# Late tiles of a routed feed-forward layer scattered into the output, and the low weights of experts 0 and 1 made by other engines

## The chip, the cores and the metric

The program runs on one core of a Trainium2 chip. The metric is the device time of one execution in microseconds; 1149.94 us is the median of three runs before the change (1149.91 to 1152.03).

## What is computed

One pre-norm decoder layer, all float32, for x of 4 x 512 x 256 tokens: a selective-scan mixer, a cross-attention over 4 x 1601 context rows, and a mixture of eight experts of which each token takes two. The change touches the last part alone, apart from two small stores.

```
scores = xt @ Wg.T                       # 2048 tokens, 8 experts
topk_scores, topk_idx = top_k(scores, 2)
y_e = (silu(xt @ W1_e.T) * (xt @ W2_e.T)) @ W3_e.T      # hidden width 704
out = x + sum over the two chosen e of score_e * y_e
```

## The kernel before, in words

The program has two parts with a barrier of all engines between them. `mixer_phase` does the mixer and the attention, batch by batch, in an order written out by hand. At its end the normalised tokens of a batch are stored to DRAM (`store_tokens`, line 303), the router's product is copied into `scores` (line 692), and SyncE waits for the stores (line 335). Near its start 5 MB of zeros are written to the DRAM tensor `ffn_sorted` (lines 269 and 270).

`routed_ffn_phase` sorts the 4096 (token, expert) pairs into 39 tiles of 128 rows, each tile of one expert, and works through the tiles. It has these pieces.

Routing. SyncE loads the weights of experts 0 and 1 (`load_expert`), ScalarE rounds each to `w_hi` (line 1236). Meanwhile VectorE runs a chain of small instructions, each of which waits for the one before (`chain`): the two best experts of each token, the place of each pair in the sorted order (`pos_f`), and one-hot matrices `place_row` and `place_tile` (lines 1335 to 1343), from which TensorE makes by 32 products the token number of each sorted row (line 1447, `tok_id`). The one-hot matrices lie in the space of `w_lo`, the low parts of the weights. So `w_lo` of expert 0 is made by VectorE only behind the routing (`split_rest(0)`, line 1394), and that of expert 1 behind the first tile's product (`split_rest(1)`). Each has a part of 2816 and one of 1536 columns.

Gathers. GpSimd fetches the 39 tiles of tokens with one indirect DMA each (line 1180). Tiles 0 to 3 are read from `tok`, later ones after a copy by SyncE into `tok_in` (`load`, line 1100), issued four tiles ahead right behind the store of a tile.

Tiles. For tile i TensorE transposes the tokens, makes gate and up products in three float32r products each (line 1478), transposes the hidden rows (lines 1487 and 1491) and makes the down product (line 1503); tile i + 1's gate and up stand in front of tile i's down. ScalarE rounds and applies silu, VectorE makes the low parts (lines 1373, 1381), the product (1367) and the copy of the result out of PSUM (`evacuate`, line 1388). SyncE stores each result to `ffn_sorted` (line 1109). The loops of TensorE, ScalarE, VectorE and SyncE are hardware loops over pairs of tiles or groups of eight.

Later experts. Behind the gathers, GpSimd waits for the last tile of expert e, makes `w_hi` and `w_lo` of expert e + 2 (lines 1151 and 1154), and issues the load of expert e + 4 (`reload`, line 1088). For experts 2 and 3 the loads are issued by SyncE, once `w_lo` of experts 0 and 1 is there.

End. A token's two rows lie at a lower and a higher place. Once all tiles up to the last of expert 6 are stored, GpSimd gathers the 16 blocks of lower rows (`fetch(y_one, 0, ...)`, line 1195); once tile 38 is stored, it gathers the 16 blocks of upper rows. VectorE multiplies each by its score and adds it to `x_all` (lines 1425, 1430), and SyncE stores pairs of blocks (line 1132).

## Time and profile before

| | |
|---|---|
| median of three runs | 1149.94 us |
| profiled execution, span from first to last instruction | 1151.0 us |
| TensorE busy over the span | 928.8 us (81%) |
| VectorE, ScalarE, GpSimd busy | 669.2, 445.6, 590.9 us |
| chain that ended last, by engine | PE 24%, DVE 3%, DMA 2%, POOL 1% |
| mean granted TensorE clock | 0.885 |

The page gives no time of the profiled execution beside its span; the span stands 1.06 us above the median. The part with the experts begins at 789 us. In the stretches of the profile PE is TensorE, PEld its weight loads, DVE VectorE, ACT ScalarE, POOL GpSimd and SP SyncE. POOL's busy time holds its making of DMA descriptors for indirect DMAs; a DMA's own time is "to landing".

### The profile page before, as it was taken

The page shows a single profiled execution, that of the slowest core. Times are in us where ns is not written, and L with a number is a line of the kernel's source. Part 1 is how long each engine was busy: PE and PEld are TensorE (multiplying, and loading weights), DVE is VectorE, ACT ScalarE, POOL GpSimd, SP SyncE. Part 2 cuts the span into 40 slices and gives each one's busy share as a digit, 9 for nine tenths or more (in the row PEclk, how much of TensorE's full clock was granted, in tenths as well). Part 3 has the DMA queues.
Part 4 walks back from the last instruction along what each step waited for, and adds up shares of the span by engine and source line. Part 5 has one row for each costly group of instructions (what it writes and reads, how often), then busy time and mean ns, then how long its engine had stood idle before and what let it go on. Part 6 is the DMA issues. An engine that isn't in the chain of part 4 may idle for free. (4 is left out here: it accounts for less than half of the span.)

```text
span 1151.0 us, 16215 instructions
## 1 busy us (share of the span) xinstructions
PE 928.8 (81%) x5148; PEld 731.9 (64%) x5149; DVE 669.2 (58%) x1097; ACT 445.6 (39%) x827; POOL 590.9 (51%) x481
## 2 busy tenths in 40 slices
PE   5767677889877889885989877992699999999970
PEld 2344345457666546665657765672689899999970
DVE  4189777697457788547677872416634343443443
ACT  2455754355544445635345530322222222222210
POOL 2176675755446565546576743110578553335505
PEclk9869877899886899996899987995699999999995
DMA  9440030000044000026000040004365312311304
GB/s 322 161 175 1 1 111 37 1 15 1 1 163 132 1 9 7 1 75 220 1 8 8 1 147 1 15 1 169 123 207 127 125 48 100 112 36 36 109 19 146
DMA packets 48954, 85.44 MB, mean 74 GB/s; under 512 B 6292, under 2 KB 38696, under 8 KB 46856
## 3 DMA queue, kind: packets, MB, share of 16 engines
q1 hardware_dynamic: 43032, 65.77, 17.0%
q0 software_dynamic: 5872, 19.02, 5.7%
q8 instruction: 29, 0.48, 0.2%
q14 instruction: 21, 0.17, 0.0%
HBM read 65.64 MB, written 14.55 MB: 70 GB/s over the span
## 5 line engine op out<-in xcount | busy, mean ns | idle before, releaser
L373 POOL TENSOR_TENSOR u<-dtx,b_all 128x512 f32<-128x512 f32 x256 | 326.6, 1288 | 212.9 <-DVE h L620 209.7
L620 DVE TENSOR_TENSOR_SCAN h<-da,u 128x512 f32<-128x512 f32 x256 | 308.6, 1217 | 136.8 <-ACT da L455 89.5
L455 ACT ACTIVATE da<-dt_,a_neg 128x512 f32<-128x512 f32 x256 | 174.8, 689 | 133.3 <-DVE h L620 132.5
L746 PE MATMUL ysum<-ident,h 128*128 128x128 f32 x1024 | 159.3, 301 | 57.9 <-DVE h L620 44.5
L746 PEld LDWEIGHTS ysum<-ident,h 128*128 128x128 f32 x1024 | 132.5, 156 | 104.2 <-DVE h L620 56.8
L924 PE MATMUL pv<-pT,ctx_n 128*128 128x128 f32 (+1 forms) x832 | 109.5, 288 | 7.6 <-DVE x_all L681 7.6
L924 PEld LDWEIGHTS pv<-pT,ctx_n 128*128 128x128 f32 (+1 forms) x832 | 104.6, 204 | 10.8 <-DVE x_all L681 9.1
L895 PE MATMUL pa<-ctx_t,xnT_a 128*128 128x401 f32 (+1 forms) x256 | 97.3, 508 | 13.9 <-DVE sim L602 12.6
L1367 DVE TENSOR_TENSOR hid<-act_,ps_u 128x352 f32<-128x352 f32 x78 | 40.6, 521 | 86.8 <-ACT act_ L1221 86.8
L1221 ACT ACTIVATE act_<-ps_g 128x352 f32<-128x352 f32 x78 | 36.3, 466 | 104.2 <-PE ps_u L1478 104.2
L1503 PE MATMUL ps_y<-w_hi,hidT_hi 128*128 x234 | 70.9, 303 | 2.7 <-DVE hidT_lo L1381 2.7
L895 PEld LDWEIGHTS pa<-ctx_t,xnT_a 128*128 128x128 f32 x256 | 44.9, 192 | 44.2 <-DVE sim L602 19.2
L729 PE MATMUL pm<-xnT_m,w_in 128*128 128x512 f32 x128 | 65.1, 637 | 6.3 <-DVE xs L576 4.8
L1503 PE MATMUL ps_y<-w_lo,hidT_hi 128*128 x234 | 66.5, 284 | 0.0
L1503 PE MATMUL ps_y<-w_hi,hidT_lo 128*128 x234 | 66.3, 283 | 0.0
L1226 ACT CAST hidT_hi<-ps_h 128x512 fp32r<-128x512 f32 x39 | 22.9, 586 | 104.3 <-PE ps_h L1491 100.1
L1180 POOL DMA_INDIRECT tok<-xn_dram,tok_id x39 | 43.9, 1125 | 35.3 <-DVE tok_id L1349 23.7
L1381 DVE TENSOR_TENSOR hidT_lo<-ps_h,hidT_hi 128x512 fp32r<-128x512 f32 (+2 forms) x117 | 42.1, 415 | 34.1 <-ACT hidT_hi L1226 34.1
L602 DVE COPY_PREDICATED sim<-mask,pa 128x401 f32<-128x401 uint8 x64 | 38.0, 596 | 37.1 <-PE pa L895 37.1
L1154 POOL TENSOR_TENSOR w_lo<-w_raw,w_hi 128x2816 fp32r<-128x2816 f32 (+1 forms) x12 | 58.6, 4882 | 0.0
L1478 PE MATMUL ps_g<-w_hi,tokT_hi 128*128 x156 | 54.6, 350 | 3.4 <-issue 3.3
L1162 POOL TENSOR_TENSOR pool_scrap<-ident 128x1 f32<-128x1 f32 x26 | 4.8, 193 | 96.3 <-PE ps_y L1503 85.3
(216 smaller groups left out, 1780.5 us busy)
## 6 DMA issues: line engine op xcount, KB each, us to landing
b_all<-b_dram SPq DMA_DIRECT2D x16, 1024.0 KB, 4.6
ctx_t<-in_ctxT SPq DMA_DIRECT2D x4, 1601.0 KB
ctx_n<-in_ctx SPq DMA_DIRECT2D x4, 1536.0 KB
ffn_sorted<-yg SPq DMA_DIRECT2D x1, 4992.0 KB, 22.5
ffn_sorted<-y_sb SPq DMA_DIRECT2D x39, 128.0 KB
tok_in<-tok SPq DMA_DIRECT2D x35, 128.0 KB, 2.0
mask<-in_mask SPq DMA_DIRECT2D x16, 200.1 KB, 2.4
w_raw<-in_w1T SPq DMA_DIRECT2D x4, 704.0 KB, 4.2
```

The costliest lines, as they stand in the source:

```text
L373: nc.gpsimd.tensor_tensor(u[:, i % 2, :], dtx[:, j % 2, :], b_all[:, n, :], ALU.mult).then_inc(u_ok, 1)
L455: nc.scalar.activation(da[i % DS][:], dt_[:, j % 2, :], ACT.Exp, scale=a_neg[:, j, n:n + 1]).then_inc(da_ok, 1)
L620: nc.vector.tensor_tensor_scan(h[:, i % HS, :], da[i % DS][:], u[:, i % 2, :], 0.0, ALU.mult, ALU.add).then_inc(scan_ok, 1)
L729: last = nc.tensor.matmul(bank[:], w_in[:, k, j * P:(j + 1) * P], xnT_m[:, k, :], start=k == 0, stop=k == KD - 1)
L746: last = nc.tensor.matmul(ysum[:, t * P:(t + 1) * P], h[:, i % HS, t * P:(t + 1) * P], ident[:], is_transpose=True, start=n == 0 and t == ...
L895: last = nc.tensor.matmul(pa[c % 2][:, 0:hi - lo], xnT_a[:, k, q * P:(q + 1) * P], ctx_t[:, k, lo:hi], start=k == 0, stop=k == KD - 1)
L924: last = nc.tensor.matmul(pv[:, k * P:(k + 1) * P], ctx_n[0:w, c, k * P:(k + 1) * P], pT[0:w, c, :], start=c == 0 and k == 0, stop=c == KC ...
L1154: nc.gpsimd.tensor_tensor(w_lo[:, p * NW + lo:p * NW + hi], w_raw[:, p, lo:hi], w_hi[:, p * NW + lo:p * NW + hi].bitcast(F32), ALU.subtrac ...
L1180: pool.indirect_dma_start(tok[:, i, :], None, xn3_dram, bass.IndirectOffsetOnAxis(ap=tok_id[:, i:i + 1], axis=0)).then_inc(tok_ld[i // 2 % ...
L1381: nc.vector.tensor_tensor(hidT_lo[0:rows_in, c:c + n, :], bank[0:rows_in, col:col + n * P].rearrange("p (c m) -> p c m", m=P), hidT_hi[0:r ...
L1478: last = nc.tensor.matmul(out[:, 0:HH], x[:, p, k * P:(k + 1) * P], w[:, at(e % 2 * NW + (first + k * HF), HH)], start=k == 0 and n == 0, ...
L1503: last = nc.tensor.matmul(ps_y[:, 0:D], x[0:rows_in, c, :], w[0:rows_in, at(e % 2 * NW + (2 * NGU + c * D), D)], start=c == 0 and n == 0, ...
```

## The change

It has these parts.

1. **Early and late tiles.** Tiles 0 to 29 are early, 30 to 38 late (`LATE = 9`). Early results go to `ffn_sorted` as before. Late results stay in `y_late` in SBUF.
2. **The scores weigh the rows.** Each token's eight scores are stored behind its 256 values in DRAM (`store_scores`, once per batch), and the gather of tokens brings them along (rows of 264 values). VectorE makes from them one weight per sorted row (`tile_masks`, `row_weights` for tiles 0 to 7 before the first result is copied out, for tiles 8 to 38 before that of tile 8) and multiplies by it while it copies a result out of PSUM. Row 0 of that DRAM tensor is zero and serves the unused rows.
3. **Early rows are added by the DMA.** Behind the store of tile 29, GpSimd issues 16 + 16 indirect DMAs that add rows of `ffn_sorted` to `x_all`. Rows that belong to late tiles are replaced by 128 rows of zeros. SyncE stores pairs of blocks to the output when both of a pair's additions have landed.
4. **Late rows are scattered.** When all eight stores have landed, GpSimd scatters late tiles from SBUF with addition into the output in DRAM: 8 DMAs for the lower rows, 9 for the upper, of which an upper one waits until the lower ones of the tiles before it have landed. Rows that don't take part go to spare rows behind the output. VectorE makes the row numbers before it copies out tile 9 (`late_rows`).
5. **Placement buffers.** `place_row` gets a buffer of its own, whose space the late buffers use afterwards, and `place_tile` lies in `hidT_hi` and `hidT_lo`.
6. **Low weights.** GpSimd makes `w_lo` of expert 0 as soon as ScalarE has rounded each part. VectorE makes that of expert 1 between the tokens of tile 0 and those of tile 1.
7. VectorE's loop over the tiles is written out; the zeros written at the start are 128 rows in place of 4992.

```diff
+LATE = 9
...
+    EARLY = NT - LATE
+
+    ffn_sorted = nc.dram_tensor("ffn_sorted", [(EARLY + 1) * P, D], F32).ap()
+    xn3_dram = nc.dram_tensor("xn3_dram", [G * P + 1, D + E], F32).ap()
...
-                sp.dma_start(env["ffn_sorted"].rearrange("(n p) d -> p n d", p=P),
-                             zeros.unsqueeze(1).to_broadcast([P, NT, D])).then_inc(res_st, 16)
+                sp.dma_start(env["ffn_sorted"][EARLY * P:(EARLY + 1) * P, :], zeros[:, 0:D]).then_inc(res_st, 16)
+                sp.dma_start(xn3_dram[0:1, :], zeros[0:1, :]).then_inc(res_st, 16)
...
+                        sp.dma_start(xn3_dram[at(b * S + t * P + 1, P), 0:D], xn[:, t, :]).then_inc(tok_st, 16)
+
+                def store_scores(b):
+                    sp.wait_ge(r_ok, b + 1)
+                    sp.dma_start(xn3_dram[at(b * S + 1, S), D:D + E].rearrange("(t p) e -> p t e", p=P),
+                                 scores[:, b * T:(b + 1) * T, :]).then_inc(score_st, 16)
...
+                        store_scores(b - 1)
+                store_scores(B - 1)
                 sp.wait_ge(tok_st, 16 * B * T)
+                sp.wait_ge(score_st, 16 * B)
...
+        tok = sb("tok", [P, NT, D + E])
...
+        with ExitStack() as placing:
+            place = buf(placing, "place", [P, 2 * G * P], F32R)
+        place_row = place[:].rearrange("p (k g m) -> p k g m", k=2, g=G)
+        place_tile = [t[:].rearrange("p c m -> p (c m)")[:, 0:G * COLS].rearrange("p (g t) -> p g t", g=G)
+                      for t in (hidT_hi, hidT_lo)]
+
+        y_late = sb("y_late", [P, LATE, D])
...
+        BATCHES = [range(LATE - 3)] + [range(t, t + 1) for t in range(LATE - 3, LATE - 1)]
+        low_st, high_st = [sem(f"low_st{n}") for n in range(len(BATCHES))], sem("high_st")
+        KNOWN = 8
...
-                for i in range(LAST, NT - AHEAD):
+                for i in range(LAST, EARLY):
                     store_and_load(i, i % GROUP)
-                for i in range(NT - AHEAD, NT):
-                    store(i, i % 2)
-                out = io["out"].rearrange("(g p) d -> p g d", p=P)
+                for i in range(EARLY, NT - AHEAD):
+                    sp.wait_ge(y_ok2, i + 1)
+                    load(i + AHEAD, (i + AHEAD) % GROUP)
+                out = io["out"][0:G * P, :].rearrange("(g p) d -> p g d", p=P)
-                    sp.wait_ge(comb, G + g + 2)
+                    sp.wait_ge(both_ld[g // 2], 64)
                     sp.dma_start(out[:, g:g + 2, :], x_all[:, g:g + 2, :]).then_inc(out_st, 16)
...
+                def split_rest(e):
+
+                    for n, (lo, hi) in enumerate(PARTS):
+                        pool.wait_ge(hi_ok, 2 * e + n + 1)
+                        nc.gpsimd.tensor_tensor(w_lo[:, e * NW + lo:e * NW + hi], w_raw[:, e, lo:hi],
+                                                w_hi[:, e * NW + lo:e * NW + hi].bitcast(F32), ALU.subtract).then_inc(w_ok, 1)
+
+                split_rest(0)
...
-                def fetch(y, k, done):
-                    for g in range(G):
-                        pool.indirect_dma_start(y[:, g, :], None, ffn_sorted,
-                                                bass.IndirectOffsetOnAxis(ap=pos[:, k, g:g + 1], axis=0)).then_inc(done(g), 16)
+
+                def add_early(k, g):
+                    pool.indirect_dma_start(x_all[:, g, :], None, ffn_sorted,
+                                            bass.IndirectOffsetOnAxis(ap=pos[:, k, g:g + 1], axis=0),
+                                            compute_op=ALU.add).then_inc(both_ld[g // 2], 16)
+
+                def add_late(k, t, done):
+                    pool.wait_ge(y_ok2, EARLY + t + 1)
+                    pool.indirect_dma_start(io["out"], bass.IndirectOffsetOnAxis(ap=late_to[:, k, t:t + 1], axis=0),
+                                            y_late[:, t, :], None, compute_op=ALU.add).then_inc(done, 16)
 
                 pool.wait_ge(pos_ok2, 1)
-
                 for p in range(2):
-                    stores = pool.value_load(tile_end[0:1, E + p:E + p + 1], min_val=1, max_val=NT)
-                    pool.wait_ge(y_st[p], stores * 16)
-                    take_wait()
-                fetch(y_one, 0, lambda g: low_ld)
-
-                for p in range(2):
-                    pool.wait_ge(y_st[p], so_far(NT - 1 if (NT - 1) % 2 == p else NT - 2, p))
-                fetch(y_two, 1, lambda g: up_ld[g // 2])
+                    pool.wait_ge(y_st[p], so_far(EARLY - 1 if (EARLY - 1) % 2 == p else EARLY - 2, p))
+                for g in range(G):
+                    add_early(0, g)
+                for g in range(G):
+                    pool.wait_ge(both_ld[g // 2], 32)
+                    add_early(1, g)
+
+                pool.wait_ge(late_ok, 1)
+                pool.wait_ge(out_st, 16 * (G // 2))
+                for n, batch in enumerate(BATCHES):
+                    for t in batch:
+                        add_late(0, t, low_st[n])
+                    if n == 0:
+                        pool.wait_ge(low_st[0], 16 * len(BATCHES[0]))
+                    else:
+                        pool.wait_ge(low_st[n - 1], 16 * len(BATCHES[n - 1]))
+                    for t in batch:
+                        add_late(1, t, high_st)
+                pool.wait_ge(low_st[len(BATCHES) - 1], 16)
+                add_late(1, LATE - 1, high_st)
+                pool.wait_ge(high_st, 16 * LATE)
...
-                chain(nc.vector.tensor_tensor(first[:, 0, :], pos_f[:, 0, :], pos_f[:, 1, :], ALU.is_lt))
-                chain(nc.vector.tensor_scalar(first[:, 1, :], first[:, 0, :], -1.0, 1.0, ALU.mult, ALU.add))
-                nc.vector.tensor_copy(pos[:], pos_f[:]).then_inc(pos_ok2, 1)
...
-                    chain(nc.vector.tensor_tensor(w_part[:, 0, :], w_top[:, 0, :], first[:, k, :], ALU.mult))
-                    chain(nc.vector.tensor_tensor(w_part[:, 1, :], w_top[:, 1, :], first[:, 1 - k, :], ALU.mult))
-                    chain(nc.vector.tensor_tensor(w_low[:, k, :], w_part[:, 0, :], w_part[:, 1, :], ALU.add))
+                    chain(nc.vector.tensor_scalar(is_late[:, k, :], pos_f[:, k, :], float(EARLY * P), None, ALU.is_ge))
+                    chain(nc.vector.tensor_scalar(to_zero[:, k, :], pos_f[:, k, :], num_f[:, 0:1], float(EARLY * P - 1),
+                                                  ALU.subtract, ALU.subtract))
+                    chain(nc.vector.tensor_tensor(to_zero[:, k, :], to_zero[:, k, :], is_late[:, k, :], ALU.mult))
+                    chain(nc.vector.tensor_tensor(pos_f[:, k, :], pos_f[:, k, :], to_zero[:, k, :], ALU.subtract))
+                nc.vector.tensor_copy(pos[:], pos_f[:]).then_inc(pos_ok2, 1)
...
-                    nc.vector.tensor_copy(y_sb[:, p, :], ps_y[:, 0:D]).then_inc(y_ok2, 1)
+                    if i < EARLY:
+                        wait(dve, y_st[p], so_far(i - 2, p))
+                    y = y_sb[:, p, :] if i < EARLY else y_late[:, i - EARLY, :]
+                    nc.vector.tensor_scalar(y, ps_y[:, 0:D], w_row[:, i:i + 1], None, ALU.mult).then_inc(y_ok2, 1)
+
+                def tile_masks():
+                    shape = [P, NT, E - 1]
+                    chain(nc.vector.memset(above[:, :, 0:1], 1.0))
+                    chain(nc.vector.memset(above[:, :, E:E + 1], 0.0))
+                    chain(nc.vector.tensor_tensor(above[:, :, 1:E], iot_f[:, 0:NT].unsqueeze(2).to_broadcast(shape),
+                                                  tend[:, 0:E - 1].unsqueeze(1).to_broadcast(shape), ALU.is_ge))
+                    chain(nc.vector.tensor_tensor(w_tile[:], above[:, :, 0:E], above[:, :, 1:E + 1], ALU.subtract))
+
+                def row_weights(lo, hi):
+                    for n in range(PAIRS):
+                        last = max(i for i in range(hi) if i // 2 % PAIRS == n)
+                        dve.wait_ge(tok_ld[n], gathered(last))
+                    chain(nc.vector.tensor_tensor(w_tile[:, lo:hi, :], w_tile[:, lo:hi, :], tok[:, lo:hi, D:D + E], ALU.mult))
+                    chain(nc.vector.reduce_sum(w_row[:, lo:hi], w_tile[:, lo:hi, :], AX_X))
+
+                def late_rows():
+                    own, late = tok[:, EARLY:NT, D:D + E], above[:, EARLY:NT, :]
+                    chain(nc.vector.tensor_scalar(low_s[:], late[:, :, 1:E + 1], OUT_OF_WAY, -OUT_OF_WAY, ALU.mult, ALU.add))
+                    chain(nc.vector.tensor_tensor(low_s[:], low_s[:], own, ALU.add))
+                    chain(nc.vector.scalar_tensor_tensor(out=high_s[:], in0=late[:, :, 0:E], scalar=-OUT_OF_WAY, in1=own,
+                                                         op0=ALU.mult, op1=ALU.add))
+                    chain(nc.vector.reduce_max(low_max[:], low_s[:], AX_X))
+                    chain(nc.vector.reduce_max(high_max[:], high_s[:], AX_X))
+                    chain(nc.vector.tensor_copy(row_id[:], tok_id[:, EARLY:NT]))
+                    chain(nc.vector.tensor_scalar(taken_by[:, 0, :], row_id[:], 1.0, None, ALU.is_ge))
+                    chain(nc.vector.tensor_tensor(taken_by[:, 1, :], low_max[:], high_max[:], ALU.is_ge))
...
+                    for k in range(2):
+                        chain(nc.vector.tensor_scalar(dump[:, k, :], num_f[:, 0:LATE], float((G + k * LATE) * P - 1), None, ALU.add))
+                        chain(nc.vector.scalar_tensor_tensor(out=away[:, k, :], in0=row_id[:], scalar=-1.0, in1=dump[:, k, :],
+                                                             op0=ALU.add, op1=ALU.subtract))
+                    chain(nc.vector.tensor_tensor(away[:], away[:], taken_by[:], ALU.mult))
+                    chain(nc.vector.tensor_tensor(away[:], away[:], dump[:], ALU.add))
+                    nc.vector.tensor_copy(late_to[:], away[:]).then_inc(late_ok, 1)
 
...
-                split_rest(0)
                 rest_of_tokens(0, 0)
+                split_rest(1)
                 rest_of_tokens(1, 1)
                 multiply(0, 0)
-                split_rest(1)
...
-                dve.wait_ge(low_ld, 16 * G)
-                for g in range(G):
-                    nc.vector.scalar_tensor_tensor(out=x_all[:, g, :], in0=y_one[:, g, :], scalar=w_low[:, 0, g:g + 1],
-                                                   in1=x_all[:, g, :], op0=ALU.mult, op1=ALU.add).then_inc(comb, 1)
-                for g in range(G):
-                    dve.wait_ge(comb, g + 1)
-                    dve.wait_ge(up_ld[g // 2], 32)
-                    nc.vector.scalar_tensor_tensor(out=x_all[:, g, :], in0=y_two[:, g, :], scalar=w_low[:, 1, g:g + 1],
-                                                   in1=x_all[:, g, :], op0=ALU.mult, op1=ALU.add).then_inc(comb, 1)
+
+                rest_of_hidden(0)
+                rest_of_tokens(2, 0)
+                multiply(1, 1)
+                tile_masks()
+                row_weights(0, KNOWN)
+                for i in range(NT):
+                    if i > 0:
+                        rest_of_hidden(i)
+                        if i + 2 < NT:
+                            rest_of_tokens(i + 2, i % 2)
+                        if i + 1 < NT:
+                            multiply(i + 1, (i + 1) % 2)
+                    if i == KNOWN:
+                        row_weights(KNOWN, NT)
+                    if i == KNOWN + 1:
+                        late_rows()
+                    evacuate(i, i % 2)
```

## Rows read from the trace of the kernel before

**Rows 1.** The windows view: busy PE, PEld, DVE, ACT, POOL; PEclk, DMA share, GB/s.

```profile
810.00:820.00 10.00, 4.01 (x18) 3.52 (x18) 8.03 (x18) 0.37 (x1) 5.45 (x3) 0.50 0.09 26
950.00:1000.00 50.00, 49.09 (x342) 46.95 (x341) 19.62 (x48) 14.47 (x42) 17.21 (x12) 1.00 0.32 113
```

**Rows 2.** The timeline of SyncE's queue; start, duration. The last row merges tiles 35 to 38.

```profile
1054.99 0.34 SPq L1109 DMA_DIRECT2D ffn_sorted<-y_sb  x1
...
1097.96 21.13 SPq L1109 DMA_DIRECT2D ffn_sorted<-y_sb  x4
```

**Rows 3.** The timeline of all engines, at the end of the program.

```profile
1118.31 0.42 DVE L1388 COPY y_sb<-ps_y 128x256 f32<-128x256 f32 x1 [4.26 <-PE ps_y L1503]
...
1120.72 1.22 POOL L1195 DMA_INDIRECT tok<-ffn_sorted,pos  x1 [35.44 <-DMA ffn_sorted<-y_sb]
...
1128.70 18.12 SPq L1132 DMA_DIRECT2D out<-x_all  x8
...
1142.60 0.96 POOL L1195 DMA_INDIRECT tok<-ffn_sorted,pos  x1 [0.30 <-issue]
```

**Rows 4.** The timeline where the second part of the program begins.

```profile
788.47 0.19 DVE L692 COPY scores<-pv 128x32 f32<-128x32 f32 x1 [5.68 <-PE pv L942]
788.94 0.38 SPq L1077 DMA_DIRECT2D w_raw<-in_w1T  x1
```

**Rows 5.** The view of DMAs: KB of each, median us from issue to landing.

```profile
out<-x_all SPq DMA_DIRECT2D x8, 256.0 KB, 2.3
...
tok<-xn_dram,tok_id POOLq DMA_INDIRECT x39, 5.2
...
w_conv<-in_w_conv SPq DMA_DIRECT2D x1, 8.0 KB, 9.6
...
tok<-ffn_sorted,pos POOLq DMA_INDIRECT x16, 2.9
```

**Rows 6.** The timeline of the routing and of the first tokens.

```profile
797.28 3.91 ACT L1236 CAST w_hi<-w_raw 128x2816 fp32r<-128x2816 f32 x2 [12.48 <-DMA w_raw<-in_w3T]
...
800.29 0.29 DVE L1317 TENSOR_TENSOR eq<-oh,slot 128x128 f32<-128x128 f32 x1
...
811.09 0.17 DVE L1347 TENSOR_TENSOR w_low<-w_part 128x16 f32<-128x16 f32 x1
...
813.45 0.20 DVE L1349 CAST tok_id<-ps_y 128x39 uint32<-128x39 f32 x1 [1.56 <-PE ps_y L1447]
...
815.90 4.74 DVE L1394 TENSOR_TENSOR w_lo<-w_raw,w_hi 128x2816 fp32r<-128x2816 f32 x2
816.64 4.83 POOL L1180 DMA_INDIRECT tok<-xn_dram,tok_id  x1 [0.30 <-issue]
...
818.93 0.37 ACT L1215 CAST tokT_hi<-ps_x 128x256 fp32r<-128x256 f32 x1 [9.70 <-PE ps_x L1465]
820.57 0.41 DVE L1373 TENSOR_TENSOR tokT_lo<-ps_x,tokT_hi 128x256 fp32r<-128x256 f32 x1
```

**Rows 7.** The timeline in the mixer, VectorE beside GpSimd.

```profile
347.60 1.26 POOL L373 TENSOR_TENSOR u<-dtx,b_all 128x512 f32<-128x512 f32 x1 [1.23 <-DVE h L620]
347.61 1.27 DVE L228 TENSOR_TENSOR ln_t<-ln_t,ln_var 128x4 f32<-128x4 f32 x1
```

**Rows 8.** The timeline of GpSimd: expert 2's first, expert 7's last low weights.

```profile
872.45 6.27 POOL L1154 TENSOR_TENSOR w_lo<-w_raw,w_hi 128x2816 fp32r<-128x2816 f32 x1
...
1050.88 3.51 POOL L1154 TENSOR_TENSOR w_lo<-w_raw,w_hi 128x1536 fp32r<-128x1536 f32 x1
```

**Rows 9.** The timeline of VectorE at expert 1's low weights and at tile 8.

```profile
829.65 4.75 DVE L1394 TENSOR_TENSOR w_lo<-w_raw,w_hi 128x2816 fp32r<-128x2816 f32 x2
...
898.52 0.42 DVE L1388 COPY y_sb<-ps_y 128x256 f32<-128x256 f32 x1 [1.43 <-PE ps_y L1503]
```

**Rows 10.** The chain of waits behind tile 0's product; start, duration.

```profile
838.34 0.44 DVE y_sb L1388
...
839.57 7.43 DMA tok_in<-tok
```

78 lines of the change are left out of this document (34 added, 44 removed).

## The prediction, made before the changed kernel ran

> **What bounds the kernel now.** The page's slices come first: TensorE is busy 9 tenths or more in nearly every slice of the expert part, with two holes, one where that part begins and one at the end. The windows view gives the same by stretch: among the tiles TensorE works 49.09 of 50 us at a granted clock of 1.00, in the routing 4.01 of 10 us at 0.50 [rows 1]. So the tiles are TensorE's, one each 7.16 us ((1097.96 - 1054.99) / 6, tile 29 to 35 [rows 2]), and the change touches no product. The timeline of the end shows the second hole: the last result leaves PSUM at 1118.31, and from 1120.72 to the end at 1151.0 GpSimd's making of 16 gathers, one each 1.26 us (0.96 and 0.30 idle), is the bound [rows 3]. The first hole is VectorE's chain from 789 to `tok_id` at 813.45, and from there to the first tile [rows 6]. Those two holes are what the change works on, and the sum is one over their edges.
>
> **The barrier between the parts.** Before, the second part starts 0.28 us after the scores' copy ends (788.66 to 788.94 [rows 4]). Now the last batch's scores are stored first and the barrier waits for their landing: 512 pieces of 32 bytes. No row shows this store. A store of 256 KB in whole rows lands in 2.3 us, and a load of 512 pieces of 16 bytes, queued behind others at the start, took 9.6 [rows 5]. I take 3.0, nearer the store, as nothing else is in flight: +3.1 with the issue, bounds +1.7 (a landing under the store's, since 16 KB is little) and +9.7. The Trainium skill (DMA: Bandwidth & Descriptors, Specifications) asks for 512 bytes a piece and says that below it the DMA reads, modifies and writes; that speaks for the upper half of this range, and no row here shows it for a store.
>
> **The routing.** GpSimd now runs `w_lo` of expert 0 while VectorE is in its chain: 6.27 and 3.51 us [rows 8], from 799.8 on, when ScalarE's first cast ends (797.28 and 2816/4352 of its 3.91 us [rows 6]). In the mixer a product of GpSimd from 347.60 to 348.86 stands beside a VectorE instruction of four elements a row with two inputs in SBUF, started at 347.61: it took 1.27 us and ended with GpSimd's [rows 7], where a link of 16 elements took 0.17 [rows 6]. So a VectorE instruction with two inputs in SBUF waits for the whole of a GpSimd instruction that reads SBUF, and most of the chain is of this form. Step by step: GpSimd takes the first part at 799.94, between two chain links, until 806.2; the link of 800.29 [rows 6] ends at 806.5 in place of 800.58 (+5.9). GpSimd's second part goes in behind that link, 806.5 to 810.0; VectorE only has a reduction (0.29) to do meanwhile, which has one input, and the next link ends 8.6 later than before. That gives +9.0 with the two links that the change takes out there (0.21 each) put back in; net of these and of the copy to `pos`, which moves behind, +8.5 for `tok_id`. The new chain links behind the one-hot matrices (8 small ones for 6, about 0.2 us each by the 0.17 of 811.09 [rows 6]) lie beside TensorE's last 16 placing products. Bounds: 0, if the two run side by side without loss, and +9.8, both parts in full.
>
> This is also where the Trainium skill speaks against the change. SBUF — State Buffer, Who interferes with whom, says that a VectorE instruction with two SBUF inputs contends with a GpSimd one that reads SBUF, and that whoever starts first keeps the shared port for its whole instruction. By that rule the step costs the 8.5 above; if each only slowed the other to half its speed, VectorE would lose some 4 to 5 in those 9.8 us. Rows 7 agree with the rule.
>
> **From `tok_id` to the first tiles.** Before, ScalarE had the tokens of tile 0 rounded at 819.30, but VectorE was in `split_rest(0)` until 820.57 [rows 6]: -1.25 with that gone. Before, `split_rest(1)` of 4.75 us [rows 9] stood between tile 0's product and its low hidden parts, and held back the first down product; now it lies beside the first gate and up products, and all its dependants but `rest_of_tokens(1)` come later than its end: another -0.85 net, so -2.1 by tile 0's result. It holds back GpSimd's gathers, as `split_rest(0)` did (4.83 for 0.96 [rows 6]), but these run ahead of their tiles.
>
> Loads follow `w_lo`. Expert 2's load now starts about 12 us ahead of the first gather and is over by it; it used to run beside the gathers. Expert 3's was issued behind `split_rest(1)`, at 834.4 (829.65 and 4.75 [rows 9]), so that the copy of tile 4's tokens, issued 839.57, took 7.43 us behind it [rows 10], and TensorE, back at 844.6 (a pitch of tiles behind tile 0), waited until 847.0. Now that load is issued about 11 us ahead of tile 0's result and over when the copy is issued, which then takes the 2 to 3 us it has elsewhere: -2.4. If it still collides, 0. The same collision near tile 9 is tied to the ends of tiles and stays.
>
> **Among the tiles.** The weighted copy out of PSUM has the shape of the old copy, 0.42 us, and reads one input from PSUM: 0. `tile_masks` and `row_weights(0, 8)` are 6 links, some 1.8 us, ahead of tile 0's result, where VectorE has 1.4 us idle behind its products [rows 9] and the next down product is 4 us off (gate and up of the next tile lie between): 0. `late_rows` is 17 links of about 0.2, so 3.5 us, in a place with the same 1.4 us idle and 4 us to TensorE's next need; GpSimd's second part for expert 3 (3.51) may hold its first link by 1.1. I take +0.5, bounds 0 and +4 (it also delays the copy of tile 13's tokens into a load). Storing the scores of earlier batches waits on SyncE ahead of a mask load that is due a third of a batch later, and the 5 MB of zeros ran beside products that waited for nothing of it: both 0. So TensorE's last tile shifts by 3.1 + 8.5 - 2.1 - 2.4 + 0.5 = +7.6.
>
> **The end.** In times of before: tile 29's store is issued at 1054.99 [rows 2]; with the 1.96 us between tile 38's store and its first gather (1118.76 to 1120.72 [rows 3]), the additions start at 1056.95. 32 at 1.26 are 40.3: 1097.3. No row shows an addition. I take GpSimd's price of a gather (0.96 and 0.30), and 4 us to land, between the 2.9 and 5.2 of the two kinds of gather [rows 5]. The last addition lands at 1100.0, its pair's store of 2.3 at 1102.8; at 1103 the scatters start. None of them can go earlier, though tiles 30 to 35 lie ready, so part of the work that was behind the last tile still is. 6 lower ones take until 1110.6, the last lands at 1113.3; 6 upper until 1121.1; lower and upper of tile 36 and lower of 37 until 1124.9; the wait for tile 36's landing and the upper of 37 until 1126.5; the last waits until 1127.8 for the lower of 37, and lands at 1132. The old tail from the landing of the last store to the end is 2.3 (18.12 after 1128.70, less a store's own 0.37, plus 2.3, against 1151.0 [rows 3, 5]): 1134.2, so -16.8. TensorE's last result, 1118.3, is 9 us off this path, which hangs on tile 29 alone; every shift of tile 29 passes through in full.
>
> **Sum.** 7.6 - 16.8 = -9.2 on the span of 1151.0, 1141.8; as the span stands 1.06 above the median, 1140.7: 1141 us.
>
> **Rivals.**
> A, as summed: 1141, with its own range 1136 to 1147. Chance 0.45.
> B, GpSimd and VectorE work side by side in the routing, if its short links and their gaps let both in: -8.5 more, 1132. For it: the granting among so short instructions isn't in any row. Against: rows 7. Chance 0.13.
> C, slower. GpSimd's making of an adding DMA is dearer than of a gather, as a destination must be read too. 49 of them stand in one chain, so an extra of 0.19 us each (9.2 / 49) eats the gain. The first gather of a group took 1.22 for 0.96 [rows 3]; at that price 49 x 0.26 = +12.7, 1153. For it: no adding DMA in the trace, and nothing in the chain has slack. Against: each moves the same 128 rows. Chance 0.23.
> D, landings are longer, 5.2 or more, since an addition reads and writes DRAM. Four stand bare (last early one, batch of six, tile 37's lower, last): 4 x 1.2 = +5, 1146; at twice that 1150. Chance 0.14.
> E, the change does not do what it says at the end: GpSimd still with expert 7's parts when tile 29 is stored (1050.88 and 3.51 [rows 8] is only 2.6 us ahead of 1056.95), or a store of small pieces near 9.6. Either alone +3 to +7: 1144 to 1148. Chance 0.05.
>
> The range that holds 8 in 10 is 1129 to 1154, from B with a better tail to C. About 0.2% (2.3 us) is what can be told from no change. A, B and E are faster, C is slower but for its cheap quarter, D is split: faster 0.75, same 0.06, slower 0.19.
>
> **What would show it.** The scores' store ahead of the second part, its first instruction about 792. VectorE instructions of 6 and 3.5 us among the chain beside GpSimd's line of `w_lo`; `tok_id` about 825, or 816.6 under B. Tile 0's result about 848, and no wait for tile 4's tokens. 32 additions on GpSimd at 1.26 from 1065, then a gap of 5 to 6 us, and a program that ends some 16 us behind TensorE. The prediction is wrong if the additions' pitch is above 1.45, or if the chain's links keep their 0.3 us beside GpSimd.

## The result, and the profile after it

The change makes the kernel slower: 1170.97 us (median of 4 runs, 1169.72 to 1172.12) against 1149.93 (median of 4, 1149.69 to 1152.03), a ratio of 1.018 with a 95% interval of 1.0165 to 1.0194. The prediction was 1141, faster, with a range up to 1154. The profiled execution took 1172.12 and spans 1170.4, against 1151.0 before: +19.4 is what the rows have to explain. The profiles used here differ by up to 2.6 us in when the first part of the program ends, also where the code up to there is the same, so the sums below are taken over stretches inside one profile.

First the page of the changed kernel, its span and its groups of GpSimd's indirect DMAs (columns: count, busy us, mean ns of one, idle time of the engine before them), with the chain that ended last ahead of the groups and the median us to landing behind them.

```profile
span 1170.4 us, 15966 instructions
...
POOL 3%; issue 1%; DMA 1%; POOLq 0%
POOL out L1240 2%; POOL x_all L1234 1%; DMA out<-y_late,late_to 1%; POOLq L1239 0%
...
L1234 POOL DMA_INDIRECT x_all<-ffn_sorted,pos x32 | 50.0, 1562 | 12.4 <-issue 9.4
L1219 POOL DMA_INDIRECT tok<-xn_dram,tok_id x39 | 40.2, 1030 | 23.7 <-DVE tok_id L1404 12.1
...
x_all<-ffn_sorted,pos POOLq DMA_INDIRECT x32, 3.8
out<-y_late,late_to POOLq DMA_INDIRECT x17, 3.7
```

Both kinds in the top groups are indirect DMAs of 128 rows from GpSimd's queue. The 39 that only gather take 1.03 us on average; the 32 that also add (L1234) take 1.56. The chain holds nothing but the adding ones. The timeline of the end shows the same in order (start us, us, engine, line; idle before in brackets):

```profile
1061.05 0.34 SPq L1139 DMA_DIRECT2D ffn_sorted<-y_sb  x1
...
1063.64 1.71 POOL L1234 DMA_INDIRECT x_all<-ffn_sorted,pos  x1 [2.98 <-DMA ffn_sorted<-y_sb]
...
1121.50 1.56 POOL L1234 DMA_INDIRECT x_all<-ffn_sorted,pos  x1 [0.30 <-issue]
...
1123.05 0.48 DVE L1445 TENSOR_SCALAR y_late<-ps_y,w_row 128x256 f32<-128x256 f32 x1 [2.95 <-PE ps_y L1584]
...
1128.60 1.60 POOL L1240 DMA_INDIRECT out<-y_late,late_to  x1 [5.54 <-issue]
...
1142.08 1.55 POOL L1240 DMA_INDIRECT out<-y_late,late_to  x1 [2.56 <-DMA out<-y_late,late_to]
...
1161.04 1.55 POOL L1240 DMA_INDIRECT out<-y_late,late_to  x1 [0.70 <-DMA out<-y_late,late_to]
```

One addition every 1.86 us (1.56 and 0.30 idle) where a gather came every 1.26 [rows 3]. The 32 additions last from 1063.64 to 1123.06. By then TensorE's last result is leaving PSUM (1123.05 against 1118.31 [rows 3]), and all 17 scatters are still to come: 47.4 us stand between that result and the end (1170.4), where before there were 32.7 (1151.0 - 1118.31).

The first hole, in the timeline of the routing; the counterparts are [rows 4, 6]:

```profile
787.43 0.19 DVE L703 COPY scores<-pv 128x32 f32<-128x32 f32 x1 [5.68 <-PE pv L953]
787.65 0.37 SPq L314 DMA_DIRECT2D xn_dram<-scores  x1
789.88 0.38 SPq L1107 DMA_DIRECT2D w_raw<-in_w1T  x1
...
801.25 9.63 POOL L1192 TENSOR_TENSOR w_lo<-w_raw,w_hi 128x2816 fp32r<-128x2816 f32 x2 [10.09 <-ACT w_hi L1293]
801.55 0.29 DVE L1375 TENSOR_REDUCE pos_f<-eq 128x16 f32<-128x128 f32 x1
801.87 5.67 DVE L1377 TENSOR_TENSOR w_part<-pos_f 128x16 f32<-128x16 f32 x1
807.57 3.35 DVE L1378 TENSOR_TENSOR pos_f<-pos_f 128x16 f32<-128x16 f32 x1
...
822.48 0.20 DVE L1404 CAST tok_id<-ps_y 128x39 uint32<-128x39 f32 x1 [0.73 <-PE ps_y L1528]
```

The reduction at 801.55, one input, runs beside GpSimd in its usual 0.29 us. The next two links have two inputs in SBUF and 16 elements a row each, and take 5.67 and 3.35. They end at 807.54 and 810.92. The row of `w_lo` merges GpSimd's two instructions, and the view of the tile `w_lo` parts them (shortest, median and longest in ns, first and last start):

```profile
L1192 POOL TENSOR_TENSOR w_lo<-w_raw,w_hi x2: 3424/4838/6252, 801.3 to 807.5; 128x2816 fp32r<-128x2816 f32 x1, 128x1536 fp32r<-128x1536 f32 x1
```

The first lasts 6.25 from 801.25, to 807.50, the second until 810.88 (801.25 and 9.63): each link ends as one of them ends. The second part of the program starts 0.94 later than before (789.88 against 788.94), and `tok_id` is made 9.03 later.

### The profile page after: what moved, and what is told of

It reads as the page before. It is cut to its first block and busy times, and to the rows that moved or that the text cites. A ratio compares the mean times of both kernels' runs of the same rounds, so it can differ in the third digit from the quotient of the medians.

```text
span 1170.4 us, 15966 instructions
## 1 busy us (share of the span) xinstructions
PE 928.0 (79%) x5148; PEld 730.3 (62%) x5149; DVE 670.2 (57%) x1088; ACT 445.3 (38%) x827; POOL 638.8 (55%) x498
## 5 line engine op out<-in xcount | busy, mean ns | idle before, releaser
L740 PE MATMUL pm<-xnT_m,w_in 128*128 128x512 f32 x128 | 67.9, 660 | 5.7 <-DVE xs L588 4.3
L1234 POOL DMA_INDIRECT x_all<-ffn_sorted,pos x32 | 50.0, 1562 | 12.4 <-issue 9.4
L1219 POOL DMA_INDIRECT tok<-xn_dram,tok_id x39 | 40.2, 1030 | 23.7 <-DVE tok_id L1404 12.1
```

What stands on the lines that cost most here:

```text
L740: last = nc.tensor.matmul(bank[:], w_in[:, k, j * P:(j + 1) * P], xnT_m[:, k, :], start=k == 0, stop=k == KD - 1)
L1234: pool.indirect_dma_start(x_all[:, g, :], None, ffn_sorted, bass.IndirectOffsetOnAxis(ap=pos[:, k, g:g + 1], axis=0), compute_op=ALU.add). ...
```

## The experiments

The first question is whether the price of an addition on GpSimd makes the end longer (theory P), or something that stays when the additions are gone (Q, as its expectation puts it). A second group asks whether the routing's delay is GpSimd's hold on the two-input links. A third uses what was found. The kernels without the additions, with halves, with the low weights behind the routing and with the low weights in the gap ran on one chip, where the kernel before took 1153.66 us (7 runs, 1148.13 to 1155.51). The other four ran on a second one (1149.58, 10 runs, 1147.07 to 1153.07). The changed kernel itself was run on neither, so what separates two versions is read from stretches of their profiles.

A second spot scatters, beside the start of the second part: between the stores of tiles 10 and 11 lie 12.67 us in the changed kernel, and 11.9, 13.1 and 9.1 in those without the additions, with halves and with 12 late tiles, which differ from it elsewhere or in the number of late tiles. So a difference of 2 us between two spans proves nothing by itself here.

The order below is by question.

**Without the additions.** The 49 indirect DMAs stay, each with its rows, but write in place of adding; this leaves out the sums of the two experts' results.

```diff
-                                            bass.IndirectOffsetOnAxis(ap=pos[:, k, g:g + 1], axis=0),
-                                            compute_op=ALU.add).then_inc(both_ld[g // 2], 16)
+                                            bass.IndirectOffsetOnAxis(ap=pos[:, k, g:g + 1], axis=0)).then_inc(both_ld[g // 2], 16)
...
-                                            y_late[:, t, :], None, compute_op=ALU.add).then_inc(done, 16)
+                                            y_late[:, t, :], None).then_inc(done, 16)
```

> The changed kernel with the additions taken out of its 49 indirect DMAs (32 of early rows, 17 of late ones): the same DMAs move the same rows but overwrite their destination, so its output leaves out the sums. Theory P (the price of making an adding DMA on GpSimd is 1.86 us against 1.26): the pitch of all 49 falls to 1.26 us, 49 x 0.60 = 29.4 us go, and the time is near 1142 us (1171.0 - 29.4). Rival Q (the pitch of 1.86 comes from where these DMAs stand, their waits and the other DMAs beside them, not from the addition): the pitch stays 1.86 and the time stays 1171 us.

Measured: 1139.63 us (1135.98 to 1141.65), ratio to the kernel before 0.9884 (0.9843 to 0.9926). Its groups and the start of its tail:

```profile
L1234 POOL DMA_INDIRECT x_all<-ffn_sorted,pos x32 | 30.6, 957 | 12.4 <-issue 9.4 <-DMA ffn_sorted<-y_sb 3.0
L1239 POOL DMA_INDIRECT out<-y_late,late_to x17 | 16.5, 972 | 12.8 <-issue 10.4 <-DMA out<-y_late,late_to 2.4
```

```profile
1061.40 1.04 POOL L1234 DMA_INDIRECT x_all<-ffn_sorted,pos  x1 [2.98 <-DMA ffn_sorted<-y_sb]
...
1129.82 0.97 POOL L1239 DMA_INDIRECT out<-y_late,late_to  x1 [0.65 <-DMA out<-y_late,late_to]
```

With the same order, the same waits and the same rows, the stretch from the first of them to the end is 77.0 us (1138.4 - 1061.40) instead of 106.8 (1170.4 - 1063.64): -29.8, and 49 x 0.6 = 29.4 is the pitch. The landings get shorter too (median 2.8 and 2.4 us for the two kinds, 3.8 and 3.7 with the additions), but of the 1.0 and 1.3, 0.6 is the making itself, and what is left changes the waits of the chain by under 1 us in sum. P holds, Q falls. The prediction's 1141 was the time of a kernel whose additions cost what gathers cost: from tile 29's store (1058.82) to the end it is 79.6 us here, and 79.2 were predicted. That closeness is partly luck, for the scatters took 2.6 less than predicted (22.2 from the first to the last, for 24.8) and the stretch behind the last 2.2 more (8.6 for 6.4).

**What the price depends on.** The first 16 additions move half the columns (512 bytes a row), the other 16 half the rows; this leaves out the rest of these sums.

```diff
+                    rows, cols = (P, D // 2) if k == 0 else (P // 2, D)
-                    pool.indirect_dma_start(x_all[:, g, :], None, ffn_sorted,
-                                            bass.IndirectOffsetOnAxis(ap=pos[:, k, g:g + 1], axis=0),
+                    pool.indirect_dma_start(x_all[0:rows, g, 0:cols], None, ffn_sorted if k else ffn_sorted.rearrange("n (h c) -> (n h) c", h=2),
+                                            bass.IndirectOffsetOnAxis(ap=pos[0:rows, k, g:g + 1], axis=0),
```

> The changed kernel in which the 16 lower early additions move rows of 128 columns (half the bytes, as many rows; they read other data), and the 16 upper ones only 64 rows of 256 columns; the output is not the reference's. Theory R (GpSimd pays for an adding DMA by the row, a descriptor each): the first 16 keep their 1.55 us each and the second 16 fall towards half of the part above a fixed cost, 0.8 to 1.2 us. Rival S (it pays by the byte): both kinds fall alike. The end comes earlier by 16 times what each kind saves.

Measured: 1169.86 us in one run. The last of the one kind and the first of the other:

```profile
1092.34 1.56 POOL L1235 DMA_INDIRECT x_all<-ffn_sorted,pos  x1 [0.30 <-issue]
1094.20 1.45 POOL L1235 DMA_INDIRECT x_all<-ffn_sorted,pos  x1 [0.31 <-issue]
```

Half the bytes save nothing (1.56), half the rows save 0.12 (1.43 to 1.45 over these 16). So from 128 rows down to 64 most of the 1.56 is a fixed price for one adding DMA, and halving rows or bytes doesn't buy it back. Fewer than 64 rows were not tried. The 0.8 to 1.2 expected for half the rows was too low, and a price by bytes falls.

The pages show one thing more, the packets of GpSimd's DMA queue (packets, MB, share of 16 engines), in the changed kernel, without the additions and with halves:

```profile
q0 software_dynamic: 11392, 21.41, 8.6%
q0 software_dynamic: 6688, 21.41, 6.3%
q0 software_dynamic: 10368, 19.32, 7.5%
```

The same megabytes take 4704 packets more with additions, 96 for each of the 49 DMAs. With halves it is 1024 fewer, 64 for each pair of one DMA with half the bytes and one with half the rows; the page doesn't say which of the two gives them. If it is the one with half the rows, 64 packets go with 0.12 us, and the 96 would be worth 0.18 of the 0.60, an estimate from these rows. What the rest is paid for is open.

**Expert 0's low weights back on VectorE, behind the routing.**

```diff
-                def split_rest(e):
-
-                    for n, (lo, hi) in enumerate(PARTS):
-                        pool.wait_ge(hi_ok, 2 * e + n + 1)
-                        nc.gpsimd.tensor_tensor(w_lo[:, e * NW + lo:e * NW + hi], w_raw[:, e, lo:hi],
-                                                w_hi[:, e * NW + lo:e * NW + hi].bitcast(F32), ALU.subtract).then_inc(w_ok, 1)
-
-                split_rest(0)
...
-                    dve.wait_ge(w_ok, 2 * e)
...
+                split_rest(0)
```

> The changed kernel with expert 0's low weights made by VectorE again, behind the routing and ahead of tile 0's tokens, as in the kernel before; the placement buffers stay where the change put them. Theory L (GpSimd's two products hold up VectorE's chain by 8.1 us): the chain's links are 0.2 to 0.3 us again, the time from the second part's start to the token numbers falls from 32.6 to about 24.5 us, 1.4 us come back because the 4.75 us of VectorE stand ahead of the tokens again, and the time falls by 6.7 us to about 1164 us. Rival M (the long links hide waits that were there anyway): under 1 us changes, or it is 1.4 us slower, 1171 to 1172 us.

Measured: 1165.81 us (1164.99 to 1170.09), ratio 1.0128 (1.0086 to 1.017). Its VectorE timeline:

```profile
789.79 0.48 DVE L1325 MEMSET w_raw<- 64x512 f32 x1 [2.44 <-PEq L253]
...
801.59 0.18 DVE L1369 TENSOR_TENSOR w_part<-pos_f 128x16 f32<-128x16 f32 x1
801.80 0.18 DVE L1370 TENSOR_TENSOR pos_f<-pos_f 128x16 f32<-128x16 f32 x1
...
813.54 0.20 DVE L1396 CAST tok_id<-ps_y 128x39 uint32<-128x39 f32 x1 [0.74 <-PE ps_y L1520]
...
816.00 4.74 DVE L1479 TENSOR_TENSOR w_lo<-w_raw,w_hi 128x2816 fp32r<-128x2816 f32 x2
```

The two held links are back at 0.18, and from VectorE's first instruction of the part to `tok_id` it takes 23.75 us, in place of 32.42 (822.48 - 790.06) in the changed kernel: GpSimd's work there cost the chain 8.7 (8.1 were expected). Some of it comes back as the 4.74 us behind `tok_id`, so the span is only 6.5 shorter (1163.9).

**GpSimd only writes.** The kernel of the last experiment, with a memset by GpSimd over 4352 columns of `w_lo` where the changed kernel has its two parts (the space is overwritten later).

```diff
+                pool.wait_ge(hi_ok, 1)
+                nc.gpsimd.memset(w_lo[:, NW:2 * NW].bitcast(F32), 0.0).then_inc(w_fill, 1)
...
```

> The changed kernel with expert 0's low weights on VectorE behind the routing, and in their old place on GpSimd one memset of the other half of that buffer (4352 columns), which reads nothing. Theory L (a VectorE instruction with two SBUF inputs waits for a GpSimd instruction because both read through one door): the chain's links beside the memset keep 0.17 to 0.29 us, the token numbers come 23.8 us after the part's start. Rival U (any GpSimd instruction on SBUF holds VectorE): a link stretches to the memset's length and the numbers come that much later. Time near 1166 us by the first.

Measured: 1167.35 us in one run. The timeline beside the memset:

```profile
801.10 3.73 POOL L1207 MEMSET w_lo<- 128x4352 f32 x1 [9.91 <-ACT w_hi L1287]
...
801.90 0.17 DVE L1371 TENSOR_TENSOR w_part<-pos_f 128x16 f32<-128x16 f32 x1
802.11 0.18 DVE L1372 TENSOR_TENSOR pos_f<-pos_f 128x16 f32<-128x16 f32 x1
802.32 2.54 DVE L1373 COPY pos_f<-w_part 128x16 f32<-128x16 f32 x1
```

The two links that took 5.67 and 3.35 beside the subtraction take 0.17 and 0.18 beside a memset, so of the two kinds tried those are held only by the one that reads SBUF. But a copy with one input, which is 0.17 elsewhere, is held until the memset ends (804.83): 2.54. So `tok_id` comes 26.12 us after VectorE's first instruction of the part, 2.4 more than without the memset, where 23.8 was expected. Theory L holds for the links with two inputs, and the one copy behaves as rival U has it. The Trainium skill (SBUF — State Buffer, Who interferes with whom) states both halves: an instruction with two SBUF inputs contends with a GpSimd instruction that reads SBUF and not with one that only writes it, and a copy can enter a mode that also takes the port pair shared with GpSimd, and can contend in it. This trace agrees with both, at the numbers above.

**Low weights in TensorE's placing gap.** VectorE makes the first part between the one-hot matrices and `tok_id`, where it waits for TensorE, and the second behind tile 0's tokens.

```diff
+                def split_rest(e, parts=(0, 1)):
...
+                split_rest(0, (0,))
...
+                split_rest(0, (1,))
```

> As the run before, but VectorE makes the first part (3.08 us) of expert 0's low weights while TensorE does its last placing products, where it had about 2.5 us idle, and the second part (1.75 us) behind tile 0's tokens. Theory L: the chain is free as in that run, of the 4.75 us at most 0.6 stay ahead of the token numbers, so about 1 us less than that run, near 1163 us. Rival M: no less than 1171 us.

Measured: 1163.76 us (1163.06 to 1164.98), ratio 1.0104 (1.0067 to 1.0141). The gap was not free: the change's own eight small links, which work out what rows the early additions fetch, already stood in it, and the low weights put behind them overran. From VectorE's first instruction of the part (789.44) to `tok_id` it took 25.92, 2.2 more than in the kernel with the low weights behind `tok_id`, not the 0.6 that was expected.

```profile
812.36 3.08 DVE L1400 TENSOR_TENSOR w_lo<-w_raw,w_hi 128x2816 fp32r<-128x2816 f32 x1
815.36 0.19 DVE L1405 CAST tok_id<-ps_y 128x39 uint32<-128x39 f32 x1
```

**The same, with those eight links and the copy to `pos` behind the tile tables.** Nobody needs them before the first late tile.

```diff
+                split_rest(0, (0,))
+                dve.wait_ge(id_mm, 1)
+                nc.vector.tensor_copy(tok_id[:], ps_y[:, 0:NT]).then_inc(id_ok, 1)
...
                 for k in range(2):
                     chain(nc.vector.tensor_scalar(is_late[:, k, :], pos_f[:, k, :], float(EARLY * P), None, ALU.is_ge))
...
                 nc.vector.tensor_copy(pos[:], pos_f[:]).then_inc(pos_ok2, 1)
-                dve.wait_ge(id_mm, 1)
-                nc.vector.tensor_copy(tok_id[:], ps_y[:, 0:NT]).then_inc(id_ok, 1)
...
```

> As the run in which VectorE makes expert 0's first low part beside TensorE's placing products, but the eight links that work out the gathered rows of early tiles, which had filled that gap, move behind the tables of tiles, where VectorE waits 3.4 us for tile 0's tokens. If the gap was full for that reason (token numbers 25.9 us after the part's start there, against 23.8 with the low part behind them), they come at 24.5 and the time falls 1.5 us, from 1163.8 to about 1162.3. If TensorE's own 16 products set that point, nothing changes: 1163.8.

Measured: 1161.32 us (1159.14 to 1162.39), ratio 1.0093 (1.0063 to 1.0122). From VectorE's first instruction of the part (789.16) to `tok_id` it took 24.04, where 24.5 was expected: the gap holds the 3.08 us nearly for nothing.

```profile
810.20 3.08 DVE L1393 TENSOR_TENSOR w_lo<-w_raw,w_hi 128x2816 fp32r<-128x2816 f32 x1
813.20 0.19 DVE L1398 CAST tok_id<-ps_y 128x39 uint32<-128x39 f32 x1
...
1050.17 0.34 SPq L1139 DMA_DIRECT2D ffn_sorted<-y_sb  x1
```

With the routing so repaired the kernel is still 11.7 us slower than before, and the loss is at the end: tile 29's store comes at 1050.17, 4.8 us ahead of the kernel before (1054.99 [rows 2]), but from it to the end it takes 109.4 us (1159.6 - 1050.17) where before there were 96.0 (1151.0 - 1054.99). -4.8 and +13.4 are the 8.6 between the two spans.

**More late tiles.** `LATE` is 12 in place of 9: the additions could start three tiles sooner, but six more scatters are made.

```diff
-LATE = 9
+LATE = 12
```

> The changed kernel with 12 late tiles in place of 9. Theory W (the additions can't start before GpSimd has made expert 7's low weights, whose last part ended at 1060.7 us, 2.9 us ahead of the first addition): the start moves 2.8 us forward only, six more scatters cost 6 x 1.86 = 11.2 us, so +8.4: about 1179 us. Rival V (the store of the last early tile sets the start, so each tile fewer brings 7.16 us and costs 3.72): -10.3, about 1161 us.

Measured: 1179.5 us (1177.18 to 1180.0), ratio 1.0247 (1.0218 to 1.0277).

```profile
1055.91 3.49 POOL L1185 TENSOR_TENSOR w_lo<-w_raw,w_hi 128x1536 fp32r<-128x1536 f32 x1
1059.56 1.71 POOL L1234 DMA_INDIRECT x_all<-ffn_sorted,pos  x1 [0.16 <-issue]
```

The first addition starts 0.16 behind GpSimd's last part of `w_lo` for expert 7, at 1059.56, only 4.1 sooner than with 9 late tiles (1063.64): the low weights gate it, not the tiles. 2.8 was expected; the rest is that GpSimd's last part itself comes 1.3 earlier in this profile. Six more adding DMAs cost 6 x 1.86 = 11.2, and from the first addition to the end it takes 118.7 us (1178.3 - 1059.56) for 106.8, +12.0. With the 4.1 that makes the +7.9 between the two spans (1178.3 - 1170.4); +8.4 was expected.

**A hybrid that pays the addition only where it is needed.** The early rows are gathered without addition into the two halves of `w_raw` (free by then), and VectorE adds them to `x_all` in tiles 32 to 36; the 17 scatters keep their addition, since `out` is already written. The routing is that of the last but one experiment, and the last scores' store no longer holds the barrier: GpSimd waits for it ahead of its first gather.

```diff
-                    pool.indirect_dma_start(x_all[:, g, :], None, ffn_sorted,
-                                            bass.IndirectOffsetOnAxis(ap=pos[:, k, g:g + 1], axis=0),
-                                            compute_op=ALU.add).then_inc(both_ld[g // 2], 16)
+                    pool.indirect_dma_start(y_two[k][:, g, :], None, ffn_sorted,
+                                            bass.IndirectOffsetOnAxis(ap=pos[:, k, g:g + 1], axis=0)
+                                            ).then_inc(both_ld[g // 2], 16)
...
+                def add(n):
+                    for _ in range(n):
...
+                        nc.vector.tensor_tensor(x_all[:, g, :], y_two[k][:, g, :], x_all[:, g, :], ALU.add).then_inc(comb, 1)
...
-                sp.wait_ge(score_st, 16 * B)
...
+                pool.wait_ge(env["score_st"], 16 * B)
```

> A version meant to beat both: the run before, and the 32 early blocks fetched by plain indirect gathers into the space of the raw weights and added by VectorE between its instructions of tiles 32 to 36, the 17 late scatters still adding; and the last scores' store is waited for by GpSimd ahead of its first gather, not by the barrier. Theory P (the price is GpSimd's, per adding DMA): 32 x 0.60 = 19.2 us less, 2.0 us less at the barrier, 1 us back for additions that wait, so 1162.3 - 20.2 = 1142 us, under the kernel before. Rival T (VectorE's additions, with two inputs in SBUF, hold up GpSimd's gathers as its low weights did, 3.2 for 0.96 us, and delay the tiles): 32 additions of 0.4 us hold it up to 13 us, 1155 us.

Measured: 1144.29 us (1143.36 to 1146.31, 7 runs), ratio to the kernel before 0.9952 (0.9934 to 0.9969). It is faster than the kernel before by 0.5%, clear of the runs' spread (its slowest of 7 is under the fastest of 10), and faster than every version that lets the DMA add the early rows. Its groups, and its timeline at the boundary and near the end:

```profile
L1229 POOL DMA_INDIRECT w_raw<-ffn_sorted,pos x32 | 32.5, 1016 | 12.5 <-issue 9.1 <-DMA ffn_sorted<-y_sb 3.0 <-DVE y_late L1451 0.3
L1235 POOL DMA_INDIRECT out<-y_late,late_to x17 | 26.4, 1554 | 13.5 <-issue 10.4 <-DMA out<-y_late,late_to 3.2
```

```profile
787.58 0.19 DVE L703 COPY scores<-pv 128x32 f32<-128x32 f32 x1 [5.68 <-PE pv L953]
...
788.62 0.38 SPq L1109 DMA_DIRECT2D w_raw<-in_w1T  x1
...
1072.46 0.95 POOL L1229 DMA_INDIRECT w_raw<-ffn_sorted,pos  x1 [0.30 <-issue]
1072.74 0.74 DVE L1508 TENSOR_TENSOR x_all<-w_raw,x_all 128x256 f32<-128x256 f32 x2
...
1073.72 1.60 POOL L1229 DMA_INDIRECT w_raw<-ffn_sorted,pos  x1 [0.30 <-issue]
1073.75 0.74 DVE L1508 TENSOR_TENSOR x_all<-w_raw,x_all 128x256 f32<-128x256 f32 x2
...
1100.08 1.64 POOL L1235 DMA_INDIRECT out<-y_late,late_to  x1 [6.11 <-issue]
```

The 32 early ones cost 32.5 us in place of 50.0. The price is back at 0.95, except for five gathers that begin while one of VectorE's additions runs or just ahead of it and take 1.15 to 1.62 (1.60 at 1073.72); one with an addition in its middle keeps 0.95 (1072.46). That is rival T, but for about 2 us in all and not 13. The part starts 0.85 after the scores' copy ends (788.62 - 787.77), against 2.26 in the changed kernel. From tile 29's store (1049.35) to the end it takes 93.1 us, 16.4 less than in the kernel with the eight links moved (109.4), where 32 x 0.60 = 19.2 were counted; the gathers held by additions are most of what is missing, and 1142 was expected in all.

## Why the prediction was wrong, step by step

In the profiled executions, beside the rows named in the prediction:

| step | predicted | measured |
|---|---|---|
| barrier and scores' store | +3.1 | +2.0 |
| routing, up to `tok_id` | +8.5 | +8.1 |
| from `tok_id` to the first tiles, with tile 4's wait | -4.5 | -4.0 |
| among the tiles | +0.5 | +1.0 |
| the scores' copy that ends the first part | 0 | -1.0 |
| tile 29's store | +7.6 | +6.06 |
| from tile 29's store to the end | 79.2 | 109.35 |

The scores' copy starts at 787.43 in place of 788.47 [rows 4]; over the ten profiles it lies between 786.5 and 789.1, so this is scatter, and its cause is open.

**The step that failed** is "No row shows an addition. I take GpSimd's price of a gather (0.96 and 0.30)". It is 1.56 and 0.30. Put in the place of 1.26, the 49 additions make 1141.8 + 29.4 = 1171.2, against a span of 1170.4. That these meet within 1 us has some luck in it, as the terms that follow and the 1.5 us by which tile 29 came earlier than predicted cancel. The 31 steps from the first addition to the last took 57.86 us (1121.50 - 1063.64) where 39.1 were counted. Among the scatters, from 1128.60 to 1161.04, it is 32.44 for 24.8: 16 steps at +0.6 make 9.6, of which 2.0 are given back since dearer issues shorten the waits for landings. The rest of the 30.1 is +0.6 ahead of the first addition and +3.0 behind the start of the last scatter (9.4 for 6.4). Of those 3.0 the making is 0.6. The other 2.4 are a second term that was sized too small, and not by the additions, since without them this stretch is 8.6: no landing of a scatter took over 3.9, so 5.4 or more lie between the last one and the program's end, where the old tail's 2.3 was taken over. No run shows what they hold. Last, the 1.06 taken off the span to get the time was of the old profile; here the median lies 0.57 above the span, another 1.6.

Rival C was this mechanism, with a chance of 0.23; only its size was off. It counted 0.26 more for each DMA, from the first gather behind the last tile (1.22), and 0.60 was outside of every bound given. That row was no price of making alone: VectorE's 16 additions for the lower rows lay beside it (6.41 us from 1118.65), and the next gather beside them took 3.65 (1122.24), so the old end wasn't one gather each 1.26 from its start, but 2.7 us longer. The text had the point from which the sign turns, 0.19 us each, and knew that nothing in the chain had slack. The error was to choose the nearest row's price for an operation that no row showed, where 49 copies of it stood in one chain, and to cut the upper bound at a price that was also a gather's.

**The barrier.** The store of 512 pieces of 32 bytes holds the second part for 2.26 us instead of 0.28: from its issue to its landing it takes about 2.0 (2.26, less 0.03 before its issue and some 0.2 for the start of the part, an estimate from these rows), near the lower bound; over the four stores the median to landing is 3.3. The Trainium skill's rule on pieces under 512 bytes (DMA: Bandwidth & Descriptors, Specifications) spoke for the upper half of the range. No price of it shows at this size: 2.0 is under the 2.3 of a store of 256 KB in whole rows [rows 5]. Whether this store read its target first is not seen.

**The routing.** Right in mechanism and size: two links waited for the whole of GpSimd's two instructions, 8.7 us by the experiment that takes them out. The links that were hit are others than named (those at 801.87 and 807.57, since ScalarE's first cast ended 1.3 us later than counted), and the reduction in between ran undisturbed, as stated. Rival B (the two engines side by side) falls, and so does the case in which each engine only slows the other.

**The first tiles.** `tok_id` was 9.03 late and tile 0's store 8.1 (847.08 against 838.95): -0.9 for the -2.1 counted. But the wait for tile 4's tokens is gone, and at tile 7 the shift is 5.0 (896.64 against 891.63). In sum it is near.

**Among the tiles.** The shift is not even: `row_weights`, one link of it held by GpSimd's next part of `w_lo`, stood in front of tile 8's result, and `late_rows` in front of tile 9's:

```profile
899.06 6.24 POOL L1185 TENSOR_TENSOR w_lo<-w_raw,w_hi 128x2816 fp32r<-128x2816 f32 x1
...
903.30 2.27 DVE L1459 TENSOR_TENSOR w_tile<-w_tile,tok 128x248 f32<-128x248 f32 x1
```

The link ends (905.57) as `w_lo` does (905.30). Stores of tiles 8 and 9 came 7.6 and 8.8 later than before, that of tile 10 6.2, that of tile 11 7.9, in the spot that scatters; by tile 29 it is 6.06. TensorE's last result is 4.7 late, and as predicted nothing depends on it.

**Rivals D and E.** Landings are 3.7 to 3.8 in the median, within the 4 us taken; D falls. (They are longer by the additions, as D says, 2.4 to 2.8 without them, but the 4 us had room for it.) Of E, GpSimd was free in time with 9 late tiles (its last part for expert 7 ends at 1060.66, the first addition starts 1063.64), but with 12 it is exactly this part that gates. The end of the program was predicted to hang on tile 29 and GpSimd alone, and it does.

## What to carry to other kernels

An operation that no row shows is the term to bound widest when many copies of it stand in one chain: compute the price at which the sign turns, and if it is a fifth of the known price, measure one before building 49. An indirect DMA that adds saves VectorE an addition of 0.37 us (0.74 for two) and costs GpSimd 0.60 more; take it only where GpSimd's queue is not the bound. Long GpSimd work that reads SBUF should lie beside matrix work, not beside a chain of tiny two-input VectorE links, where two parts of 6.25 and 3.42 us cost the chain 8.7.

## What the runs showed of the hardware that was not expected

- Making an indirect DMA with an addition takes GpSimd 1.55 to 1.57 us, without it 0.95 to 0.97 (the first one or two of a row of them up to 1.71 and 1.04), with 0.30 between two in both cases. 512 bytes a row in place of 1024: 1.56; 64 rows in place of 128: 1.44. Reading from DRAM into SBUF with addition (1.56) and writing to DRAM with addition (1.55) cost the same. Why an addition is dearer to make was not found (each makes 96 packets more, which by the estimate above would be 0.18 of the 0.60).
- VectorE with two inputs in SBUF holds GpSimd's making of an indirect DMA. The prediction had one case of it (4.83 [rows 6]); here gathers of tokens beside VectorE's 4.74 us of `w_lo` took 4.85 and 4.70 in place of 0.97 in the kernel with the low weights back on VectorE, and one of the hybrid's took 1.60 beside two additions of 0.37. What is new is where they end: those three end 0.83 to 0.84 us behind VectorE's instructions (821.57 for 820.74, 826.58 for 825.74, 1075.32 for 1074.49), and so does the one of 3.65 in the kernel before (1125.89 for 1125.06). That is most of the making's own 0.95: a gather that begins beside VectorE's work is made nearly whole behind it, and one that has begun earlier goes on (1072.46). VectorE's instructions keep their length (2816 columns of `w_lo` take 3.08 with and without a gather beside them).
- A GpSimd memset doesn't hold VectorE's two-input links (0.17 each) but holds a one-input copy of 16 elements for 2.54 us.
